# Scan passes over one image in two directions instead of two images in one, with rows repeated by single transfers from device memory

## The chip, the cores and the metric
One NeuronCore of a Trainium2 chip runs the whole program. Its engines are TensorE (PE; its weight loads are shown apart, as PEld), VectorE (DVE), ScalarE (ACT), GpSimd (POOL) and SyncE (SP), which here only issues DMAs. Each engine runs its own instructions in order, and they wait for each other on semaphores. Sixteen DMA engines serve the core. The metric is the device time of one execution in microseconds (us), and the median of several runs is compared.

## What is computed
The input is x, four images of 16 by 16 pixels with 192 channels, float32. First comes a layer with a selective scan (after a normalisation of x in groups of 6 channels), then attention with positive features over 12 heads, then a layer in which a router picks 6 of 12 heads per image; each adds to x. The scan layer is the part that changes:

```
xz = x @ in_proj_w.T;  xh, z = split(xz)             # 96 channels each
xc = silu(depthwise_conv3x3(xh) + conv_b)
xs = rows order, columns order, and both reversed    # K = 4 directions of L = 256 steps
dts, Bs, Cs = split(xs @ x_proj_w[k].T)              # 12, 16 and 16 rows
d = softplus(dts @ dt_projs_w[k].T + dt_projs_b[k])
h = h * exp(d_t * A) + (d_t * u_t) * B_t             # 96 channels x 16 states, for t = 0 .. 255
y_t = sum over states of h * C_t, plus D * u_t
y = the four directions turned back and added; then layer norm, * silu(z), @ out_proj_w.T
```

The outputs are the four images after all three layers.

## The kernel before
**Passes and units.** The scan runs in eight passes (`SCANS`), numbered n: two halves of two images each (`HALVES`, `IMG`), times the four directions. A pass holds its two images side by side, 512 columns. A unit u is a twelfth of a pass (`UNITS`): 8 channels by 16 states on the 128 partitions. There are 96 units. In unit u:
- PE's `spread_out` multiplies a 0/1 matrix with `stack` (the step d and the input d*u, each as a sum of three bf16 numbers hi, mid and lo), which repeats each channel's row over its 16 states: `step_bc` for the decay, `inp_bc` for the drive, each in two PSUM banks.
- ACT's `expo` makes the decay exp(a * d) from `step_bc` (L732), three buffers.
- DVE's `drive_of` multiplies `inp_bc` with `b_rep`, the repeated rows of B (L1010), and `scan` runs the recurrence over the 512 columns (L1019) into one of four `state` buffers.
- POOL's `weigh` multiplies the states with `c_rep` (L559), three `outp` buffers, and PE's `sum_states` adds over the states into `y_acc` (L1397). After twelve units DVE's `add_y` adds `y_acc` to `y_sum` in the direction's order (L1034, L1037, L1044).

**Preparation.** Around the start of pass n, at fixed units (`PRE_RAW` to `PRE_LO`), the next pass is prepared: PE's `pre` (L1374), ACT's `pre_raw` (L699, L704), clip on DVE (L976), exponential and logarithm on ACT (L710, L712), `pre_ln`, `pre_max` and `pre_max_series` (L980, L984, L989), the product with the input (L997), casts on ACT (`hi`, `mid`, L720, L724), subtractions on POOL (L544, L549). SP's queue copies `bc` sixteen times per pass into `b_rep` and `c_rep` (L433) and `hi`, `mid` and `lo` nine times into `stack` (L446). POOL's `orders` writes the three other directions of `xs`.

**Before the loop** the first half is normalised, projected and convolved on DVE (L955, L958), one image after the other, and gated (L962); the second half's convolution goes through PE in the loop.

**Steps beside the units.** `side_work` is a planner: it places the steps of the later layers (`ATTN_STEPS`, `HEAD_STEPS`, `FFN_STEPS`; 34 for each image) in lists `beside[u]`, by costs `PE_COST` and a room of `PE_ROOM` per unit. PE does them in unit u, the other engines one unit later (`LAG`). What doesn't fit stands in `rest` and follows the loop: image 0 and 1 may start after 48 units, images 2 and 3 after all 96. Here `rest` holds 91 steps. The steps named later: `yT` (the scan's sum turned), `q0` to `q2`, `kv00` to `kv11` (features), `hT`, `lg` and `cr` (router), `fq`, `fk`, `fv`, `s0`, `s1` (scores), `t0`, `t1` (probabilities turned), `w0`, `w1` (values weighed), `fo` and `rn` (end of an image).

```
            for u in range(SLOT_COUNT):
                expo(u)
                ...
                for item in beside[u - LAG] if u >= LAG else []:
                    side(*item)
```

Of the kernel before, what the change touches and what calls it, by code (L numbers as in the profile page):

```python
# [24 lines left out]
P = 128  # L25
IMAGES, SIDE, CH = 4, 16, 192
L = SIDE * SIDE
HALVES = 2
IMG = IMAGES // HALVES
TOK = IMG * L  # L30
TILES = TOK // P
CK = CH // 2
DI, NS, RANK, DIRS = 96, 16, 12, 4
GRP = P // NS
UNITS = DI // GRP
CHUNK = 32
CHUNKS = DI // CHUNK
PER_CHUNK = CHUNK // GRP
# [7 lines left out]
RING = 3  # L46
SLOTS = 3
STATE_SLOTS = 4
# [10 lines left out]
PRE_HI, PRE_REST, PRE_MID, PRE_LO = (2, 3), (4, 5), (5, 6), (6, 6)  # L59
SECOND_LATER = 3  # L60
LOG_MAX = 82.0

CONST2 = 3 + 1 + HPC + TOPK
ONES = 13
BEHIND = (0, 0, 0, 6)
FIRST_STEP = 4
ADD_Y = 3
Z_GATED = 2
ACC_ROWS = IMG * (SIDE + 2) - 2
SCANS = HALVES * DIRS  # L70
# [6 lines left out]
HEAD_STEPS = ["s0", "t0", "s1", "w0", "t1", "w1"]  # L77
# [17 lines left out]
def side_work():  # L95

    beside = [[] for _ in range(SLOT_COUNT)]

    for at, step in FRONT_BESIDE:
        beside[at].append((step, 1))  # L100
    for i, step in enumerate(WEIGHT_STEPS):
        beside[WEIGHTS_FIRST + 2 * i].append((step, 0))
# [3 lines left out]
    done, ready = [0, 0], [DIRS * UNITS + FIRST_STEP, DIRS * UNITS + FIRST_STEP + 1]  # L106
    for u in range(DIRS * UNITS, SLOT_COUNT):
        held = 0.0
        for n in (0, 1):
            if ready[n] > u or done[n] >= (len(steps) if n == 0 else done[0]):  # L110
                continue
            step = steps[done[n]]
            if step in HEAD_STEPS and (n % IMG or step == "w0"):
# [8 lines left out]
    at = {step: i for i, step in enumerate(steps)}  # L122
    done += [0, 0]
    rest = []
    while min(done) < len(steps):
        for n in range(IMAGES):
            if done[n] == len(steps) or (n and done[n - 1] < min(len(steps), done[n] + 1 + BEHIND[n])):
                continue
            if n >= IMG and (done[n] == at["tT"] and done[n - IMG] <= at["fv"] or done[n] == at["un"] and done[n - IMG] <= at["fo"]):
                continue  # L130
            rest.append((steps[done[n]], n))
            done[n] += 1
# [3 lines left out]
def products(step, n):  # L136
# [7 lines left out]
    if step in HEAD_STEPS:  # L144
        heads = range(int(step[1]), TOPK, 2)
        return {"s": [f"s{n}{j}" for j in heads], "t": [f"pt{n}{j}" for j in heads], "w": [f"pv{n}", f"pd{n}"] * (step == "w0")}[step[0]]
# [11 lines left out]
def ring_plan():  # L158

    beside, rest = side_work()  # L160
    names = ["w_in", "gm0", "w_xp", "w_dt", "gv0", "w_alog", "xh0_0", "xh1_0", "w_fold", "gm1", "z_0", "gv1", "d0"]
# [9 lines left out]
    for i, name in enumerate(names):  # L171
        if name[:2] in ("pv", "pd"):
            at = FINAL_RING - 2 + (name[1] == "d")
        else:
            at = turn % (RING if i < early else FINAL_RING - 2)
            turn = turn + 1 if i + 1 != early else 0
# [5 lines left out]
def hybrid_kernel(nc, x, in_proj_w, conv_w, conv_b, x_proj_w, dt_w, dt_b, A_logs, Ds, norm_g, norm_b, out_proj_w,  # L182
# [5 lines left out]
    with ExitStack() as ctx:  # L188
# [31 lines left out]

        step_bc = [ctx.enter_context(nc.psum_tensor(f"step_bc{i}", [P, TOK], F32)) for i in range(2)]
        inp_bc = [ctx.enter_context(nc.psum_tensor(f"inp_bc{i}", [P, TOK], F32)) for i in range(2)]
        y_acc = ctx.enter_context(nc.psum_tensor("y_acc", [P, TOK], F32))
        banks = [ctx.enter_context(nc.psum_tensor(f"ring{i}", [P, TOK], F32)) for i in range(RING)]
        banks += step_bc + inp_bc + [y_acc]

        def bank(name):
# [3 lines left out]
        x_tok = sb("x_tok", [P, HALVES * TILES, CH])  # L231
# [12 lines left out]
        spread = sb("spread", [DI, PER_CHUNK, P], BF16)  # L244
# [17 lines left out]
            "room_b", [([CK, 2, HALVES * TOK], F32), ([FEAT, HPC, FEAT], F32), ([FEAT, HPC, HD], F32), ([CK, HPC, FEAT], F32)],  # L262
            [([P, PAIRS, TOK], F32)])
        valr = sb("valr", [1, IMG, 3 * HEADS, HD])
        acc, opw, hn = shared("room_e", [([DI, ACC_ROWS, SIDE], F32), ([CK, 2, DI], F32)], [([P, TILES, CH], F32)])
# [3 lines left out]
                                                        ([DIRS * UNITS, P], F32)], [([P, TILES, DI], F32)],  # L269
                                             [([P, TILES, CH], F32)])  # L270
        sg, gT = shared("room_i", [([DI, TOK], F32)], [([DI, TOK], F32)])

        stack, prob1, probT1 = shared("room_s", [([DI, 2, CHUNKS, 2 * TOK], BF16)],
                                      [([P, PER_ROUND, 2, L], F32), ([P, PER_ROUND, 2, L], F32)])
        prob = [sb("prob0", [P, PER_ROUND, 2, L]), prob1]
        probT = [sb("probT0", [P, PER_ROUND, 2, L]), probT1]


        fq = [sb("fq0", [CK, 2, L])]
# [1375 lines left out]
```

## Time and profile before
| | |
|---|---|
| median of 3 runs | 461.55 us (460.12 to 461.58) |
| the profiled execution | 463.01 us, of which the profile's span is 461.3 us |
| PE, share of the span | 371.3 us, 80% |
| DVE | 346.4 us, 75% |
| POOL | 206.9 us, 45% |
| ACT | 179.8 us, 39% |
| DMA | 12.69 MB in 15743 packets, mean 28 GB/s |

The profile shows the instructions of each engine with start, duration, source line (L12 is line 12 of the kernel) and the idle time before them, with what ended it. Durations come from one execution. "State" is the scan's output, "room_g" and the like are names of shared memory: room_g holds `xs` and later results, room_s `stack`, room_a the keys' features, room_e the convolution's sums, room_i the gate, room_h and room_f inputs of steps.

### The profile page before, as it was taken

To read this page: it belongs to the slowest core of one execution; us is meant where nothing else is said; L and a number is where in the kernel's file an instruction comes from. 1 tells how busy PE (TensorE), PEld (TensorE's weight loads), DVE (VectorE), ACT (ScalarE), POOL (GpSimd) and SP (SyncE) were. 2 spreads that over 40 slices of the span, in tenths; PEclk is the share of its full clock that TensorE was granted. 3 is DMA by queue.
4 is the path that set the end of the run, shared out by engine and by line. 5 is a ranking of instruction groups with operands and counts; after the bars stand their busy time and mean duration, and the time that the engine had idled before them with its cause. 6 is when DMAs were issued, how large, how long until landed. Compare 5 with 4: busy or idle time off the path is not lost. (4 is left out here: it accounts for less than half of the span.)

```text
span 461.3 us, 5553 instructions
## 1 busy us (share of the span) xinstructions
PE 371.3 (80%) x1669; PEld 214.3 (46%) x1669; DVE 346.4 (75%) x622; ACT 179.8 (39%) x405; POOL 206.9 (45%) x210
## 2 busy tenths in 40 slices
PE   5825499697887867857999998896989999969691
PEld 4612133142332312323557555553865786958450
DVE  5885989878999999999789898987457356263514
ACT  2565354554563534423243332335225211135340
POOL 7131697867895967774653863451121010000001
PEclk9999889979897987785999999999799989588966
DMA  5502212011121110110101010000000000000000
GB/s 121 106 21 64 56 26 64 23 41 34 23 58 34 47 40 18 40 43 9 47 21 33 11 34 1 0 2 1 2 17 1 1 0 17 2 1 1 1 17 18
DMA packets 15743, 12.69 MB, mean 28 GB/s; under 512 B 7279, under 2 KB 11361, under 8 KB 15713
## 3 DMA queue, kind: packets, MB, share of 16 engines
q1 hardware_dynamic: 15713, 12.33, 11.7%
q8 instruction: 14, 0.23, 0.2%
q14 instruction: 16, 0.13, 0.1%
HBM read 2.62 MB, written 0.79 MB: 7 GB/s over the span
## 5 line engine op out<-in xcount | busy, mean ns | idle before, releaser
L559 POOL TENSOR_TENSOR outp<-state,c_rep 128x512 f32<-128x512 f32 x96 | 126.4, 1321 | 93.0 <-PE y_acc L1397 43.1
L1019 DVE TENSOR_TENSOR_SCAN state<-decay,inp_bc 128x512 f32<-128x512 f32 x96 | 117.2, 1221 | 9.3 <-DVE inp_bc L1010 4.3
L1397 PE MATMUL y_acc<-outp,band 128*96 128x512 f32 x192 | 111.2, 666 | 6.7 <-DVE y_sum L1034 2.6
L732 ACT ACTIVATE decay<-step_bc,a_neg 128x510 f32<-128x510 f32 x96 | 64.9, 683 | 47.0 <-PE step_bc L1384 46.8
L1010 DVE TENSOR_TENSOR inp_bc<-b_rep,inp_bc 128x512 f32<-128x512 f32 x96 | 65.5, 682 | 7.1 <-PE inp_bc L1388 6.9
L1388 PE MATMUL inp_bc<-room_s,spread 96*128 96x512 bf16 x96 | 41.0, 427 | 31.1 <-DVE state L1019 31.0
L494 POOL TENSOR_TENSOR rs<-mv,neg_half 128x2 f32<-128x2 f32 x16 | 11.1, 696 | 120.0 <-DVE mv L1055 119.9
L1384 PE MATMUL step_bc<-room_s,spread 96*128 96x512 bf16 x96 | 39.9, 415 | 12.7 <-DMA room_s<-lo 11.6
L1397 PEld LDWEIGHTS y_acc<-outp,band 128*96 128x96 f32 x192 | 34.3, 182 | 24.7 <-issue 10.3
L1388 PEld LDWEIGHTS inp_bc<-room_s,spread 96*128 96x128 bf16 x96 | 9.9, 103 | 65.9 <-DVE state L1019 56.8
L1384 PEld LDWEIGHTS step_bc<-room_s,spread 96*128 96x128 bf16 x96 | 10.4, 109 | 32.5 <-issue 27.3
L720 ACT CAST hi<-step 96x512 bf16<-96x512 f32 x16 | 9.9, 616 | 33.4 <-DVE step L989 24.7
L1507 PE MATMUL ring<-kvw,tT 96*128 96x480 f32 (+1 forms) x48 | 21.2, 567 | 0.0
L1132 DVE RECIPROCAL spl<-y_acc 96x256 f32<-96x256 f32 x4 | 7.0, 1754 | 15.4 <-PE y_acc L1436 15.4
L1125 DVE TENSOR_REDUCE nmax<-ring 128x2 f32<-128x512 f32 x19 | 12.0, 680 | 7.1 <-PE step_bc L1407 3.9
L1501 PE MATMUL ring<-tT,qw 96*128 96x256 f32 (+1 forms) x64 | 16.6, 404 | 0.8 <-issue 0.8
L544 POOL TENSOR_TENSOR step<-step,hi 96x512 f32<-96x512 f32 x14 | 16.1, 1151 | 0.0
L549 POOL TENSOR_TENSOR lo<-step,mid 96x512 bf16<-96x512 f32 x14 | 15.9, 1154 | 0.0
L1501 PEld LDWEIGHTS ring<-tT,qw 96*128 96x128 f32 (+1 forms) x64 | 12.8, 202 | 5.9 <-issue 4.3
L724 ACT CAST mid<-step 96x512 bf16<-96x512 f32 x16 | 9.9, 616 | 13.6 <-POOL step L544 13.4
L1525 PEld LDWEIGHTS ring<-cbd,room_b 128*128 128x128 f32 x96 | 13.7, 227 | 1.0 <-issue 1.0
L1525 PE MATMUL ring<-cbd,room_b 128*128 128x34 f32 x96 | 13.6, 307 | 0.0
(346 smaller groups left out, 650.8 us busy)
## 6 DMA issues: line engine op xcount, KB each, us to landing
b_rep<-bc SPq DMA_DIRECT2D x64, 32.0 KB, 1.9
c_rep<-bc SPq DMA_DIRECT2D x64, 32.0 KB, 2.0
room_s<-hi SPq DMA_DIRECT2D x24, 64.0 KB, 2.0
room_s<-mid SPq DMA_DIRECT2D x24, 64.0 KB, 2.0
room_s<-lo SPq DMA_DIRECT2D x24, 64.0 KB, 2.0
x_tok<-in_x_dram SPq DMA_DIRECT2D x2, 384.0 KB, 3.8
out_dram<-room_g SPq DMA_DIRECT2D x4, 192.0 KB, 2.0
room_a<-in_L_attn_w_qkv_dram SPq DMA_DIRECT2D x1, 432.0 KB, 6.5
```

Source lines behind the costliest of these rows:

```text
L544: g.tensor_tensor(step2[:, i, :], step2[:, i, :], hi[:, i, :], ALU.subtract).then_inc(S["rest"], 1)
L549: g.tensor_tensor(lo[:, i, :], step2[:, i, :], mid[:, i, :], ALU.subtract).then_inc(S["lo"], 1)
L559: g.tensor_tensor(outp[:, u % SLOTS, :], state[:, u % STATE_SLOTS, :], c_rep[:, n % 2, :], ALU.mult).then_inc(S["outp"], 1)
L732: a.activation(decay[:, u % SLOTS, :, 1:L], step_bc[u % 2][:, :].rearrange("p (b l) -> p b l", b=IMG)[:, :, 1:L], ACT.Exp, scale=a_neg[:, ...
L1010: v.tensor_tensor(inp_bc[u % 2][:, :], b_rep[:, n % 2, :], inp_bc[u % 2][:, :], ALU.mult).then_inc(S["drive"], 1)
L1019: v.tensor_tensor_scan(state[:, u % STATE_SLOTS, :], decay[:, u % SLOTS, :, :].rearrange("p b l -> p (b l)"), inp_bc[u % 2][:, :], 0.0, AL ...
L1384: t_.matmul(step_bc[u % 2][:, :], spread[:, q, :], stack[:, n % 2, j, 0:TOK], start=True, stop=True).then_inc(S["bc_step"], 1)
L1388: t_.matmul(inp_bc[u % 2][:, :], spread[:, q, :], stack[:, n % 2, j, TOK:2 * TOK], start=True, stop=True).then_inc(S["bc_inp"], 1)
L1397: t_.matmul(y_acc[0:DI, :], band[:, at:at + DI], outp[:, u % SLOTS, :], start=(g12 == 0), stop=(g12 == UNITS - 1)).then_inc(S["y_mm"], 1)
L1501: ins = t_.matmul(b_[:, u * L:(u + 1) * L], qw[0:CK + c, c, i * P:(i + 1) * P], tT[0:CK + c, c, at0:at0 + L], start=(c == 0), stop=(c == 1))
L1507: ins = t_.matmul(b_[:, 0:w], tT[0:CK + c, c, at:at + P], kvw[0:CK + c, c, j, :], start=(c == 0), stop=(c == 1))
L1525: ins = t_.matmul(b_[:, at:at + w], qp[:, i, at0 + t * P:at0 + (t + 1) * P], cbd[:, b, i, :], start=True, stop=True)
```

## The change
A pass is now one image read in row order and in column order, side by side (`WAYS`), and its two backward directions are the next pass: eight passes again, image 0 forward, image 0 backward, image 1 forward and so on. For a backward pass the decay and the scan are read from the last column to the first, and only the column order is made by `orders`. A unit is 16 channels by 8 of the 16 states (`SN`), twelve a pass again: six with the lower states, six with the upper.

The step and the input (`step2`, float32, no splitting) are written by SP's queue to `step_rows` in device memory, once a pass, and each unit's 16 rows come back by one transfer that repeats each 8 times (`in_rep`, four slots). C goes through `c_rows` likewise, two transfers a pass. B comes repeated out of a product, `fill_b`, into two banks `b_bc`. `spread_out`, `stack`, the casts and the subtractions are gone. The drive has one bank, `drv`; the decay two buffers. The ring of banks has four instead of three in the loop and all eight after it. Image n's later steps may start from unit 24(n+1)+4, and many steps wait one unit instead of two for their predecessor. `prob` and `probT` exist once instead of twice, and `w0` and `w1` are one step `w`. `rest` now holds 64 steps instead of 91.

```diff
-HALVES = 2
-IMG = IMAGES // HALVES
+IMG = 2
+WAYS = 2
-GRP = P // NS
-UNITS = DI // GRP
+SN = 8
+GRP = P // SN
+GROUPS = DI // GRP
+PARTS = NS // SN
+UNITS = PARTS * GROUPS
+PER_IMAGE = DIRS // WAYS
-RING = 3
+RING = 4
 SLOTS = 3
+IN_SLOTS = 4
+DECAY_SLOTS = 2
-BEHIND = (0, 0, 0, 6)
+BEHIND = (0, 0, 0, 0)
...
-UNITS_AFTER = {step: 1 for step in ("q0", "q1", "q2", "kv00", "kv01", "kv10", "wqk", "wv", "fq", "fk")}
+UNITS_AFTER = {step: 1 for step in ("gT", "tT", "q0", "q1", "q2", "kv00", "kv01", "kv10", "kv11", "cx", "aT", "hT", "wqk", "wv", "fq", "fk", "fv", "t0")}
...
+    ready = [PER_IMAGE * UNITS * (n + 1) + FIRST_STEP for n in range(IMAGES)]
+    for u in range(PER_IMAGE * UNITS, SLOT_COUNT):
...
+            def keep_c(n):
+                taken(sp, f"d{n}")
+                sp.dma_start(c_rows[n % 2].rearrange("i s t -> (i s) t"), step2[DI:, 0, :]).then_inc(S["c_kept"], 16)
+            def repeat_c(n, i):
+                sp.wait_ge(S["c_kept"], 16 * (n + 1))
+                if n:
+                    sp.wait_ge(S["outp"], UNITS * (n - 1) + GROUPS * (i + 1))
+                sp.dma_start(c_rep[:, i, :], c_rows[n % 2, i].unsqueeze(0).to_broadcast([GRP, SN, TOK])).then_inc(S["c_there"][i], 16)
+            def keep_step(n):
+                sp.wait_ge(S["step"], n + 1)
+                if n >= 2:
+                    sp.wait_ge(S["decay"], UNITS * (n - 1))
+                sp.dma_start(step_rows[n % 2], step2[0:DI, :, :].rearrange("p a t -> p (a t)")).then_inc(S["step_kept"], 16)
+            def repeat_step(u):
...
+                if u % UNITS == 0:
+                    sp.wait_ge(S["step_kept"], 16 * (n + 1))
+                if u >= IN_SLOTS:
+                    sp.wait_ge(S["decay"], u - IN_SLOTS + 1)
+                    sp.wait_ge(S["drive"], u - IN_SLOTS + 1)
+                rows = step_rows[n % 2, GRP * g:GRP * (g + 1), :]
+                sp.dma_start(in_rep[:, u % IN_SLOTS, :, :].rearrange("p a t -> p (a t)"),
+                             rows.unsqueeze(1).to_broadcast([GRP, SN, 2 * TOK])).then_inc(S["in_there"][u % IN_SLOTS], 16)
...
             def expo(u):
-                act.wait_ge(S["bc_step"], u + 1)
-                if u >= SLOTS:
-                    act.wait_ge(S["state"], u - SLOTS + 1)
...
+                act.wait_ge(S["in_there"][slot], 16 * (u // IN_SLOTS + 1))
+                if u >= DECAY_SLOTS:
+                    act.wait_ge(S["state"], u - DECAY_SLOTS + 1)
+                kept = slice(0, L - 1) if back else slice(1, L)
+                for e in range(WAYS):
+                    at = (part * DIRS + WAYS * back + e) * GROUPS + c16
+                    ins = a.activation(decay[:, back, u % DECAY_SLOTS, e, kept],
+                                       in_rep[:, slot, 0, :].rearrange("p (e l) -> p e l", e=WAYS)[:, e, kept],
+                                       ACT.Exp, scale=a_neg[:, at:at + 1])
...
             def drive_of(u):
...
-                dve.wait_ge(S["bc_inp"], u + 1)
-                v.tensor_tensor(inp_bc[u % 2][:, :], b_rep[:, n % 2, :], inp_bc[u % 2][:, :],
-                                ALU.mult).then_inc(S["drive"], 1)
...
+                dve.wait_ge(S["in_there"][slot], 16 * (u // IN_SLOTS + 1))
+                if u:
+                    dve.wait_ge(S["state"], u)
+                v.tensor_tensor(drv[:, :], in_rep[:, slot, 1, :], b_bc[part][:, :], ALU.mult).then_inc(S["drive"], 1)
```

**The queue of SP**, at the start of the loop. Before, from the repeats of B for the first pass on:

```order
L433 DMA b_rep<-bc 16x512 x8
L446 DMA room_s<-hi 32x1024
L446 DMA room_s<-mid 32x1024
L446 DMA room_s<-lo 32x1024
L433 DMA c_rep<-bc 16x512 x8
```

With the change, the first pass's rows and the first units:

```order
L441 DMA c_rows<-step 16x512
L455 DMA step_rows<-step 96x1024
L467 DMA in_rep<-step_rows 128x1x1024 x2
L448 DMA c_rep<-c_rows 128x1x512 x2
L467 DMA in_rep<-step_rows 128x1x1024 x5
L441 DMA c_rows<-step 16x512
L467 DMA in_rep<-step_rows 128x1x1024 x3
L455 DMA step_rows<-step 96x1024
```

The copies between parts of SBUF have become a write to device memory and one wide read a unit, and the next pass's rows are written between the reads of this one.

**PE at the end of the loop.** Before, the last unit's sums, and then the first steps of `rest` (room_e and y_sum are the inputs of hT of image 1 and yT of image 2):

```order
L1407 MATMUL ring<-fk,fq 128x256 x6
L1397 MATMUL y_acc<-outp,band 96x512 x4
L1419 MATMUL ring<-ident,prob 128x128 x12
L1447 MATMUL step_bc<-ident,room_e 96x128 x4
L1481 MATMUL step_bc<-ident,y_sum 128x96 x2
```

With the change (the scores before the loop's end are image 1's, y_sum is the input of yT of image 3):

```order
L1369 MATMUL y_acc<-outp,band 96x512
L1474 MATMUL ring<-tT,qw 128x256 x4
L1369 MATMUL y_acc<-outp,band 96x512 x3
L1391 MATMUL ring<-ident,prob 128x128 x12
L1474 MATMUL ring<-tT,qw 128x256 x4
L1454 MATMUL b_bc<-ident,y_sum 128x96 x2
```

Image 0 is finished in the loop, image 1 stands where image 0 stood, and image 2 is already at its third query product.

## Rows read from the trace of the kernel before

**Rows 1.** Stretches of the execution: length, busy time of each engine (instructions), PE clock, DMA

```profile
40.27:311.03 270.76, 227.02 (x773) 106.54 (x772) 244.48 (x335) 112.91 (x215) 178.84 (x150) 0.90 0.14 32
311.03:461.29 150.26, 124.29 (x822) 93.34 (x820) 73.42 (x210) 47.15 (x147) 13.48 (x18) 0.85 0.02 6
...
138.00:170.00 32.00, 23.96 (x65) 8.66 (x63) 31.21 (x33) 13.59 (x23) 23.35 (x19) 0.84 0.17 40
```

**Rows 2.** Timeline of DVE, units with nothing between: start, duration, line, operation

```profile
119.43 1.22 DVE L1019 TENSOR_TENSOR_SCAN state<-decay,inp_bc 128x512 f32<-128x512 f32 x1
120.57 0.68 DVE L1010 TENSOR_TENSOR inp_bc<-b_rep,inp_bc 128x512 f32<-128x512 f32 x1
121.28 1.22 DVE L1019 TENSOR_TENSOR_SCAN state<-decay,inp_bc 128x512 f32<-128x512 f32 x1
```

**Rows 3.** Waits in the loop, DVE's: us in total, times, longest

```profile
DVE inp_bc L1010 <- PE inp_bc L1388: 6.9, 8, 3.2
...
DVE state L1019 <- ACT decay L732: 2.0, 4, 1.0
```

**Rows 4.** Timeline of PE after the loop, with idle time before and its releaser

```profile
314.74 1.53 PE L1419 MATMUL ring<-ident,prob 128*128 128x128 f32 x12 [1.16 <-DVE y_sum L1044]
...
346.30 2.00 PE L1501 MATMUL step_bc<-tT,qw 96*128 96x256 f32 x8 [0.16 <-DVE room_f L1072]
```

**Rows 5.** Stretches after the loop, columns as in rows 1

```profile
311.03:346.30 35.27, 29.03 (x204) 21.72 (x202) 21.70 (x70) 12.31 (x39) 5.75 (x8) 0.90 0.02 7
346.30:461.29 114.99, 95.25 (x618) 71.62 (x618) 51.72 (x140) 34.84 (x108) 7.74 (x10) 0.83 0.02 6
```

**Rows 6.** Groups of DVE in the loop: busy us, mean ns, idle before

```profile
L984 DVE TENSOR_TENSOR step<-step,spl 96x512 f32<-96x512 f32 x7 | 10.3, 1466 | 0.0
...
L989 DVE TENSOR_TENSOR step<-step,sps 96x512 f32<-96x512 f32 x7 | 4.8, 679 | 0.0
...
L1044 DVE TENSOR_TENSOR y_sum<-y_sum,y_acc 96x256 f32<-96x256 f32 x6 | 3.2, 581 | 0.5 <-PE y_acc L1397 0.5
...
L1034 DVE SCALAR_TENSOR_TENSOR y_sum<-room_g,dsum,y_acc 96x512 f32<-96x512 f32 x2 | 1.5, 739 | 0.1
...
L1037 DVE TENSOR_TENSOR y_sum<-y_sum,y_acc 96x512 f32<-96x512 f32 x2 | 1.3, 674 | 0.0
```

**Rows 7.** The page's groups: a spread product of PE

```profile
L1388 PE MATMUL inp_bc<-room_s,spread 96*128 96x512 bf16 x96 | 41.0, 427 | 31.1 <-DVE state L1019 31.0
```

**Rows 8.** Timelines of ACT and DVE at a kv step

```profile
229.39 0.24 ACT L783 COPY v<-ring 128x96 f32<-128x96 f32 x1 [2.65 <-DVE room_a L1166]
229.53 0.69 ACT L732 ACTIVATE decay<-step_bc,a_neg 128x510 f32<-128x510 f32 x1
...
230.30 1.22 DVE L1019 TENSOR_TENSOR_SCAN state<-decay,inp_bc 128x512 f32<-128x512 f32 x1 [0.40 <-DVE inp_bc L1010]
```

**Rows 9.** Timelines of DVE and ACT before the first unit

```profile
15.93 4.10 DVE L958 SCALAR_TENSOR_TENSOR room_e<-room_w,cw,room_e 96x256 f32<-96x256 f32 x8
...
25.87 0.42 DVE L962 TENSOR_TENSOR room_g<-room_e,room_i 96x256 f32<-96x256 f32 x1 [0.40 <-ACT room_i L671]
...
34.31 1.41 DVE L1002 TENSOR_TENSOR step<-step,hi 96x512 f32<-96x512 f32 x2
...
40.27 0.69 DVE L1010 TENSOR_TENSOR inp_bc<-b_rep,inp_bc 128x512 f32<-128x512 f32 x1 [3.18 <-PE inp_bc L1388]
...
20.59 0.42 ACT L669 ACTIVATE room_i<-room_i 96x256 f32<-96x256 f32 x1
```

**Rows 10.** Short stretches at the start, columns as in rows 1

```profile
3.00:4.00 1.00, 0.00 (x0) 0.00 (x0) 0.86 (x2) 0.00 (x0) 1.00 (x3) 1.00 1.07 359
9.00:11.50 2.50, 2.27 (x12) 1.90 (x11) 0.59 (x4) 0.47 (x1) 1.05 (x2) 1.00 0.63 65
```

**Rows 11.** The page's DMA issues: count, KB each, us from issue to landing

```profile
room_s<-hi SPq DMA_DIRECT2D x24, 64.0 KB, 2.0
...
x_tok<-in_x_dram SPq DMA_DIRECT2D x2, 384.0 KB, 3.8
```

More of the change, by code:

```diff
@@ L126, in side_work @@
         for n in range(IMAGES):
[L127 to L132, printed above, removed]
+            if may_go(n):
+                rest.append((steps[done[n]], n))
+                done[n] += 1
     return beside, rest
@@ L144, in products @@
     if step in HEAD_STEPS:
-        heads = range(int(step[1]), TOPK, 2)
-        return {"s": [f"s{n}{j}" for j in heads], "t": [f"pt{n}{j}" for j in heads], "w": [f"pv{n}", f"pd{n}"] * (step == "w0")}[step[0]]
+        heads = [] if step == "w" else range(int(step[1]), TOPK, 2)
+        return {"s": [f"s{n}{j}" for j in heads], "t": [f"pt{n}{j}" for j in heads], "w": [f"pv{n}", f"pd{n}"]}[step[0]]
     return [f"{step}_{n}"]
@@ L663, in _ @@
[L663 to L674 removed]
+            act.wait_ge(S["conv"], 9)
@@ L676, in weights @@
+            for n in range(1, IMAGES):
+                group_normed(n)
+            for n in range(1, IMAGES):
+                pad(n)
             def weights(step):
@@ new lines, in collected, with group_deviations @@
+            def collected(first, last, count):
+                dve.wait_ge(S["gn_stats"], count)
+                for s in range(2 * first, 2 * last):
+                    v.bn_aggr(gmv[:, s, :], gst[:, s, :]).then_inc(S["gn_agg"], 1)
+            def group_deviations(i, cols):
+                w = cols.stop - cols.start
+                fetched(dve, f"gm{i}")
+                dve.wait_ge(S["gn_agg"], cols.stop)
+                v.tensor_copy(gmean[:, cols], bank(f"gm{i}")[0:CK, 0:w]).then_inc(freed(f"gm{i}"), 1)
+                taken(dve, f"gm{i}")
+                v.tensor_tensor(gdv[:, cols], gmv[:, cols, 0], gmean[:, cols], ALU.subtract).then_inc(S["gn_dev"], 1)
+                dve.wait_ge(S["gn_dev"], 2 * i + 1)
+                v.tensor_tensor(gsq[:, cols], gdv[:, cols], gdv[:, cols], ALU.mult).then_inc(S["gn_dev"], 1)
+                dve.wait_ge(S["gn_dev"], 2 * i + 2)
+                v.tensor_tensor(gva[:, cols], gsq[:, cols], gmv[:, cols, 1], ALU.add).then_inc(S["gn_var"], 1)
@@ L913, in _ @@
+            group_bias(0, one)
+            turned_stats(2, 1)
+            for c in range(2):
+                turned_stats(3, c)
+            collected(1, IMAGES, 2 * IMAGES)
             for e in range(2):
@@ new lines, in pre, with fill_b @@
+            def pre(n):
+                b_ = begin(f"d{n}")
+                for e in range(WAYS):
+                    ins = way(b_, n, e)
+                done(ins)
+            def fill_b(n, part):
+                if n:
+                    pe.wait_ge(S["drive"], UNITS * (n - 1) + GROUPS * (part + 1))
+                i = n // PER_IMAGE
+                pe.wait_ge(S["xs"], i + 1)
+                for e in range(WAYS):
+                    k = WAYS * (n % PER_IMAGE) + e
+                    ins = t_.matmul(b_bc[part][:, e * L:(e + 1) * L], w_b[:, k, part, :], xs[:, i, e, :], start=True, stop=True)
+                ins.then_inc(S["b_there"], 1)
@@ L1595, in side @@
                     done(ins)
-            front("z", 0)
+            for n in range(1, IMAGES):
+                inner(n)
             b_ = begin("d0")
```

803 lines of the change are left out of this document (350 added, 453 removed).

## The prediction

> **What bounds the kernel now.** I read first the three stretches into which the first and the last scan cut the execution [rows 1, 9]: 40.3 us before the first drive, 270.8 us in which the 96 units run, 150.3 us after the last scan. In the middle stretch VectorE (DVE) is busy 244.5 of 270.8 us, no other engine over 227. In the last it is busy 73.4 of 150.3 and TensorE (PE) 124.3: the loop belongs to DVE, the end to PE. The timeline of DVE shows the smallest unit: drive 0.71 us to the scan, scan 1.14 us to the next drive, 1.85 us, with the drive starting 0.08 us before the scan's end [rows 2]. 96 of these are 178 us; the rest of the loop is preparation of the next pass and steps of the later layers, woven between the units. The waits of DVE in the loop come third: 6.9 us for the bc product that PE makes, little for the decay [rows 3].
>
> **The end.** This carries the gain. Before, the layers behind the scan may start for two images only after 48 units; now image n starts after 24(n+1). What PE has left after the loop falls from 91 steps to 64 by the planner. The new list starts with the turning of image 1's probabilities, q2 of image 2 and yT of image 3. The old list reaches exactly this state (yT of image 3 just done) when PE starts q2 of image 2, at 346.30 [rows 4]. From there to the end it took 115.0 us, PE busy 95.3 of it [rows 5]. Between the last scan's end, 311.03, and PE's first step, 314.74 [rows 4], 3.7 us went into the last product, sum and add_y, which stay. I add 2 us, since fk and fv of image 3 now run with no other image's work beside them, and nothing for the changed banks. New end: 3.7 + 115.0 + 2 = 120.7, so 150.3 becomes 120.7: **-29.6 us**. Bounds: -33 (more banks let PE run on) and -22 (PE's mean granted clock was 0.83 of full speed here [rows 5]; a lower one stretches it).
>
> **The loop.** It starts and ends with the same 96 units of 128x512. Terms on DVE:
> - The steps that leave the end enter the loop. The old end did them from 311.03 to 346.30, with DVE busy 21.7 us [rows 5]; +21.7.
> - Drive u+1 now waits until scan u has finished, since there is one drv where there were two banks. An instruction that waits for its predecessor starts 0.03 us after its end (scan after drive), one that doesn't starts 0.08 before it [rows 2]: 0.12 a unit where nothing stands between. By the plan 27 of the 95 changes of unit are such; +3.3. Bounds 0 and 11.4 (all 95).
> - add_y: in the loop ten instructions, 3.2 + 1.5 + 1.3 = 6.0 us [rows 6]. Now three images by about 0.48 + 0.58: -2.8. A memset of 0.5 goes to POOL, the gate of image 1 (0.5) comes in from the start: 0.
> - PE makes no more spread products, two a unit; B comes from one product for half a pass. The 6.9 us of waits for inp_bc [rows 3] go. PE is no more near its limit: these products (96 by 0.43 us [rows 7], and 96 of the other kind, taken as equal) are some 82 of its 227 us.
> - POOL loses 28 subtractions, ACT 28 casts: neither bounds, so nothing in the sum by itself. What DVE loses to POOL is visible: the maximum with spl takes 1466 ns on average, its twin with sps 679 [rows 6], 5.5 us in all. I take that it stays, as POOL's products still run beside it.
> - ACT reads the decay's exponent from SBUF in two instructions of 255 columns. One of 256 took 0.42 [rows 9], one of 510 0.69 [rows 8]; the pair costs about 0.8, 0.1 more, and lies on the path only where ACT waits for DVE first. That is seen at the kv steps: ACT's copy waits for DVE's, the exponential comes behind it, and the scan starts 0.40 us after its drive [rows 8]. Eight such steps: +1. The same happens at the heads' scores (three maxima on DVE, six exponentials and then the decay on ACT), which come into the loop three times, and at their two weighings: +5 together, at 1 us each. Bounds 0 and 15, as decay now has two buffers and ACT can be only one unit ahead.
>
> Sum: 21.7 + 3.3 - 2.8 - 6.9 + 6 = **+21.3 us**; the loop is then 292 us, 3.04 a unit.
>
> The transfers are to hide in this. Each unit reads 16 rows of 4 KB from device memory, each eight times: 524 KB, where the passes before moved 12.7 MB in all. No row shows such a transfer. From above: loading x ran at 359 GB/s [rows 10], or 1.5 us a unit. From below: while the vectors that repeat one row over 128 partitions were loaded, 65 GB/s moved at a busy share of 0.63 [rows 10], 103 if full, or 5.1 us a unit. I take 260 GB/s, 2.0 us: here 16 different rows are read at once, one by each DMA engine, which is nearer to x than to one row for all. Then the 16 DMA engines are busy two thirds of the loop, and four buffers, freed when decay and drive are done, leave four units (7.9 us at least) for issue, landing and exponential, 5 us. Hidden, at nothing. Without this cover each us beyond the unit's own 3.04 costs 96 us. SP issues one a unit (0.5 us) in order; the repeat of C waits behind POOL's product of two units ago, done by then.
>
> **The start.** With one image instead of two before the first pass, the gate that ended at 26.29 [rows 9] ends when the first convolution (to 20.0), three exponentials and logarithms of 0.42 and one product of 0.42 are done, at 21.9: -4.4. The product of the second way now waits for POOL's reordering: +0.7. From the finished step (34.31, where the splitting starts) to the first drive (40.27) it took 5.96 us: splits on DVE, stack, spread. Now a write of 384 KB (3.0, between 2.0 for 64 KB and 3.8 for 384 KB [rows 11]), then a read of 512 KB (4.0, as the larger of these and a little), with 0.2 of waits: 7.2, +1.2. **Start -2.5 us**; bounds -5 and +2.
>
> On these two transfers the Trainium skill, "DMA: Bandwidth & Descriptors", section on measured bandwidth, would give 2.0 us and the bytes at 436 GB/s, an estimate of 2.9 and 3.2 us: the sum would be 1 us lower. By its section on latency (device memory answers in 2 us instead of 0.2 at high load) it would be some 4 us higher. No row here shows either. On the long maximum, "SBUF — State Buffer" (rules on the shared port) says that a VectorE instruction with two SBUF inputs is held up by a GpSimd one that reads SBUF; the trace agrees, 1466 against 679 ns. By that rule, with 28 POOL instructions fewer, up to 5.5 us more could go.
>
> **Sum**: -2.5 + 21.3 - 29.6 = -10.8 us. The profiled execution took 463.01 (span 461.3), so 452.2 for such a one; the median of the runs is 461.55, so **450.8 us**.
>
> **Rivals.**
> 1. *The transfers set the pace; slower.* At in_rep. It decides when 524 KB need more than 3.04 us, under 172 GB/s. At 150 GB/s a unit is 3.5 us, the loop 336, 66 more than now: 461.55 - 2.5 + 66 - 29.6 = 495 us. For it: the rows that repeat one line run at 103 GB/s when full. Against: 359 GB/s for x, in shorter runs. Chance 0.15. If writes into SBUF slowed the engines it would look alike, but the skill's SBUF page says that DMA and engines cannot contend, and no row here tells.
> 2. *The stalls go; faster still.* From 138 to 170 us DVE is busy 31.2 of 32.0 [rows 1]. With that share, work of 244.5 + 21.7 + 3.3 - 2.8 = 266.7 takes 273 us instead of 292: 432 us. For it: most idle time of DVE waits for PE's queue, which empties, and part of the 5.5 us of the long maximum can go with POOL's subtractions. Against: steps now stand one unit apart and wait for each other across engines. Chance 0.15.
> 3. *ACT and the heads eat the gain.* Decay two deep, two instructions a unit, three images' copies in the loop: with 10 to 20 us of stalls more, 461 to 471. For it: the 0.40 us at each kv step. Against: ACT is busy 113 of 271 us. Chance 0.12.
> 4. *The scan read backwards costs more.* Half of the units do so. At half as long again, 48 by 0.61 = 29 us: 480. Against: the sum that reads y_acc backwards took 674 ns for 512 columns like any other [rows 6]. Chance 0.05.
>
> **How the numbers follow.** Forecast 0.53, rivals 0.15, 0.15, 0.12, 0.05. The range takes the forecast with its bounds, rivals 2 to 4: 432 to 480. Left out are rival 1 and the edge of 2. What this measurement can tell from no change is about 0.3%, 1.4 us. Faster: 0.53 + 0.15 + 0.04 of rival 3 = 0.72; same 0.04 (rival 3); slower 0.04 + 0.15 + 0.05 = 0.24.
>
> **What would show it.** Right: last scan some 120 us before the end; 96 units in 285 to 300 us; DVE over 88% busy between; first scan at 38 to 39; drive-to-drive 1.97 us where nothing lies between; transfers landing in under 5 us, with hardly a wait for in_rep on ACT or DVE. Wrong: ACT's or DVE's waits named in_rep, in tens of us; an end that still takes 130 us or more; scans of over 1.3 us in odd passes.

## The result and the profile after

The changed kernel takes 480.94 us (median of 4 runs, 479.27 to 482.1), the kernel before in the same session 461.56 (460.12 to 463.07): ratio 1.042, 95% interval 1.037 to 1.046. It is slower by 19 us. The forecast was 450.8 us, faster; the result lies just above the upper end of the range, 480. Medians here are over all runs of a kernel; the ratios leave out slow executions, four of ten in e2_warm and two of four in e6_later, without which these two medians are 461.1 and 487.7 us.

The profiled execution took 479.27 us, of which the span is 477.5. First the stretches of the changed kernel, cut at its first drive and its last scan as in [rows 1, 5] (columns as there), with a second set of cuts inside the end:

```profile
0.00:43.63 43.63, 23.30 (x95) 17.16 (x95) 18.52 (x66) 15.30 (x37) 10.51 (x37) 0.94 0.42 90
43.63:337.42 293.79, 225.56 (x864) 129.81 (x864) 261.09 (x391) 135.94 (x344) 151.45 (x125) 0.86 0.77 194
337.42:477.50 140.08, 113.86 (x639) 85.57 (x636) 54.53 (x151) 35.25 (x108) 10.16 (x13) 0.77 0.02 5
...
337.42:348.10 10.68, 8.86 (x44) 5.79 (x41) 3.70 (x8) 3.86 (x9) 1.72 (x2) 1.00 0.00 1
348.10:477.50 129.40, 105.00 (x599) 79.78 (x598) 50.83 (x144) 31.39 (x99) 8.44 (x11) 0.75 0.02 5
```

The three stretches had been forecast at 37.8, 292 and 120.7 us. They are 43.6, 293.8 and 140.1. So the loop came out within 1.7 us, the start missed by 5.9 us and the end by 19.4. Together that is 27.0 of the 30.1 us between 450.8 and 480.94; the rest lies in which executions were profiled, above the median before (463.01) and below it after (479.27).

**The loop.** DVE is busy 261.1 of 293.8 us (0.89). The timeline of DVE, where nothing stands between units, answers to [rows 2] (L991 is the drive now, L1002 the scan):

```profile
90.68 0.70 DVE L991 TENSOR_TENSOR drv<-in_rep,b_bc 128x512 f32<-128x512 f32 x1
91.41 1.22 DVE L1002 TENSOR_TENSOR_SCAN state<-decay,drv 128x512 f32<-128x512 f32 x1
92.73 0.70 DVE L991 TENSOR_TENSOR drv<-in_rep,b_bc 128x512 f32<-128x512 f32 x1
93.46 1.22 DVE L1002 TENSOR_TENSOR_SCAN state<-decay,drv 128x512 f32<-128x512 f32 x1
```

A drive now starts 0.10 to 0.11 us behind the scan's end and a bare unit takes 2.05 us, not 1.97. All 96 scans, backward or forward, take the same: the next row gives smallest, median and largest in ns. The rows under it are DVE's and ACT's longest waits in the loop, as in [rows 3].

```profile
L1002 DVE TENSOR_TENSOR_SCAN state<-decay,drv x96: 1219/1220/1222, 44.6 to 336.2; 128x512 f32<-128x512 f32 x96
```

```profile
DVE state L1002 <- DVE drv L991: 6.7, 10, 1.0
DVE state L1002 <- ACT decay L731: 5.9, 8, 2.4
...
ACT decay L731 <- DVE state L1002: 54.3, 35, 5.0
...
ACT decay L731 <- DMA in_rep<-step_rows: 25.1, 13, 11.2
```

Of ACT's 25.1 us for in_rep, 11.2 are the very first unit. The reads of a unit landed 5.0 us after their issue (median, the page's DMA issues):

```profile
in_rep<-step_rows SPq DMA_DIRECT2D x96, 512.0 KB, 5.0
```

**The start.** The gate ends at 22.63 us (forecast 21.9). The first steps are then late: timelines of PE and of ACT.

```profile
23.90 4.89 PE L1256 MATMUL ring<-room_b,room_f 96*96 96x256 f32 x12 [5.82 <-ACT room_b L630]
28.63 1.03 PE L1342 MATMUL ring<-xs,pre_w 96*112 96x256 f32 x4
```

```profile
24.55 1.01 ACT L630 ACTIVATE room_b<-y_acc,gbi,grs 96x256 f32<-96x256 f32 x2
...
28.88 0.37 ACT L616 COPY room_c<-ring 96x256 f32<-96x256 f32 x1 [0.82 <-PE ring L1256]
29.69 0.83 ACT L708 ACTIVATE step<-ring,dtb 96x256 f32<-96x256 f32 x2 [0.44 <-PE ring L1342]
```

The product of the first pass (`d0`, L1342) stands on PE behind the projections of images 1 to 3 (L1256), and on ACT its copy (L708) stands behind their normalisation and their copies.

**The end.** The mean granted clock of PE is 0.75 of full speed from 348.10 on, where it was 0.83 over the same steps in the kernel before. Short windows show two levels, 1.00 and 0.50, and that it stays at the lower one for long:

```profile
346.00:366.00 20.00, 17.73 (x115) 10.34 (x114) 12.35 (x35) 5.85 (x17) 2.68 (x4) 1.00 0.00 1
366.00:379.00 13.00, 13.00 (x56) 12.23 (x56) 1.90 (x6) 1.06 (x3) 0.99 (x1) 0.50 0.04 15
380.00:391.00 11.00, 10.85 (x47) 6.86 (x44) 6.67 (x20) 1.79 (x7) 0.70 (x1) 1.00 0.00 0
394.00:416.00 22.00, 22.00 (x88) 18.78 (x89) 3.27 (x13) 2.19 (x12) 0.00 (x0) 0.50 0.00 0
```

What PE did before the first fall is in its timeline:

```profile
361.74 1.78 PE L1480 MATMUL ring<-kvw,tT 96*128 96x480 f32 x4
365.46 4.77 PE L1488 MATMUL b_bc<-v,room_a 128*128 128x34 f32 x24 [1.94 <-ACT v L780]
370.04 1.07 PE L1417 MATMUL b_bc<-ident,room_h 128*96 128x128 f32 x4
370.92 5.30 PE L1498 MATMUL drv<-cbd,room_b 128*128 128x34 f32 x24
376.03 3.76 PE L1474 MATMUL y_acc<-tT,qw 96*128 96x256 f32 x8
```

PE paused for 1.94 us, waiting for ACT's copy of v ahead of `cx` of image 2, and then 24 products of 34 columns took 4.77 us. (`cx`, L1488, multiplies the keys' features with v into the attention's context; `at`, L1498, multiplies the queries' features with that; `cr`, L1528, turns the router's values.) In the kernel before this step came without a pause and took 2.87 us:

```profile
366.30 2.87 PE L1515 MATMUL step_bc<-v,room_a 128*128 128x34 f32 x24
```

The second long stretch at the lower level, from 394, follows a pause of 1.73 us ahead of `cr` of image 2. Four shorter ones, the last from 458 us, come the same way, each behind a pause of 0.85 to 2.04 us.

### The profile page after: what moved, and what is told of

It is laid out like the page before. It is cut to its first block and busy times, and to the rows that moved or that the text cites. A ratio compares the mean times of both kernels' runs of the same rounds, so it can differ in the third digit from the quotient of the medians.

```text
span 477.5 us, 5515 instructions
## 1 busy us (share of the span) xinstructions
PE 362.7 (76%) x1595; PEld 232.5 (49%) x1595; DVE 334.1 (70%) x606; ACT 186.5 (39%) x489; POOL 172.1 (36%) x174
## 5 line engine op out<-in xcount | busy, mean ns | idle before, releaser
L1002 DVE TENSOR_TENSOR_SCAN state<-decay,drv 128x512 f32<-128x512 f32 x96 | 117.2, 1220 | 16.7 <-DVE drv L991 6.7
L731 ACT ACTIVATE decay<-in_rep,a_neg 128x255 f32<-128x255 f32 x192 | 86.2, 503 | 79.8 <-DVE state L1002 54.3
L991 DVE TENSOR_TENSOR drv<-in_rep,b_bc 128x512 f32<-128x512 f32 x96 | 66.1, 688 | 12.7 <-DMA in_rep<-step_rows 10.1
L534 POOL TENSOR_TENSOR rs<-mv,neg_half 128x2 f32<-128x2 f32 x16 | 11.2, 698 | 146.0 <-DVE mv L1029 146.0
L1359 PEld LDWEIGHTS b_bc<-xs,w_b 96*128 96x128 f32 x64 | 13.9, 217 | 10.4 <-issue 8.4
L1359 PE MATMUL b_bc<-xs,w_b 96*128 96x256 f32 x64 | 18.7, 421 | 0.0
L1391 PE MATMUL ring<-ident,prob 128*128 128x128 f32 x76 | 13.8, 332 | 6.3 <-ACT prob L752 3.7
L1391 PEld LDWEIGHTS ring<-ident,prob 128*128 128x128 f32 x76 | 10.8, 172 | 10.6 <-ACT prob L752 5.3
L616 ACT COPY room_c<-ring 128x512 f32<-128x512 f32 (+1 forms) x23 | 11.7, 566 | 10.5 <-PE ring L1391 5.6
L1430 PE MATMUL ring<-room_c 96*96 96x256 f32 x54 | 13.0, 381 | 1.5 <-ACT qw L616 1.0
L1535 PE MATMUL ring<-sel_m,fT 96*96 96x96 f32 (+1 forms) x64 | 10.1, 342 | 5.0 <-DVE sel_u L1178 5.0
```

What stands on the lines that cost most here:

```text
L731: ins = a.activation(decay[:, back, u % DECAY_SLOTS, e, kept], in_rep[:, slot, 0, :].rearrange("p (e l) -> p e l", e=WAYS)[:, e, kept], AC ...
L991: v.tensor_tensor(drv[:, :], in_rep[:, slot, 1, :], b_bc[part][:, :], ALU.mult).then_inc(S["drive"], 1)
L1002: v.tensor_tensor_scan(state[:, u % STATE_SLOTS, :][:, order], held[:, order], drv[:, :][:, order], 0.0, ALU.mult, ALU.add).then_inc(S["st ...
L1359: ins = t_.matmul(b_bc[part][:, e * L:(e + 1) * L], w_b[:, k, part, :], xs[:, i, e, :], start=True, stop=True)
L1391: ins = t_.transpose(b_[:, (2 * kt + q) * P:(2 * kt + q + 1) * P], prob[:, j // 2, q, kt * P:(kt + 1) * P], idn)
L1430: ins = t_.matmul(b_[0:DI, 0:L], taps[:, i, :], xpad[:, n, i // 3:i // 3 + SIDE, i % 3:i % 3 + SIDE], start=(i == 0), stop=(i == 8))
```

## The experiments

The theory after this reading: the end missed because PE's pauses let the clock fall (the order of the steps leaves a pause just ahead of long stretches of narrow products), and the start missed because of the order of two queues. The rivals: the clock falls with the narrow products, whatever stands ahead of them; the transfers hold the loop; the moved steps gain nothing.

**Order of the start.** `names` is the order in which PE makes the products ahead of the loop; `inner(n)` is the projection of image n (`xh_n`).

```diff
-    names = [..., "w_fold", "xh_1", "xh_2", "xh_3", "d0"]
+    names = [..., "w_fold", "d0", "xh_1", "xh_2", "xh_3"]
...
-            for n in range(1, IMAGES):
-                inner(n)
             b_ = begin("d0")
...
+            for n in range(1, IMAGES):
+                inner(n)
             pe.wait_ge(S["const2"], CONST2)
```

On ACT `pre_raw(0)` and `pre_softplus(0)` likewise go ahead of `group_normed` and `pad` of images 1 to 3, on POOL the clearing of wsel behind `orders(0)`.

> The product of the first step (d0) and ScalarE's copies of it go ahead of the projections and normalisations of images 1 to 3, and GpSimd's clearing of wsel behind the reordering of image 0. If the start is long because the first pass waits behind the other images' work in the queues of PE and ACT: the first drive moves from 43.6 to about 38 us, loop (293.8) and end (140.1) stay, 475 to 476 us. Rival, the moved work is paid in the first units: first drive at 38, but a loop of 297 to 300, 479 to 481 us.

475.12 us (473.0 to 475.79), 5.8 us less by the medians. First drive at 39.2 (some 38 had been expected), loop 294.8, end 140.1. PE makes the first pass's product 5.4 us earlier than in the changed kernel:

```profile
23.26 2.02 PE L1342 MATMUL ring<-xs,pre_w 96*112 96x256 f32 x4 [4.72 <-DVE xs L950]
```

The first drive comes 4.4 us earlier. In the other runs here that leave the start's order alone it comes at 43.6 to 45.4 us, so this gain is clear of that spread.

**Pauses filled.** `warm` repeats a product of `ident` with itself into the bank that the step has just taken; the step's own product, or transpose, overwrites it.

```diff
+            WARM = {"cx_2": 9, "cr_2": 8, "cx_3": 4, "cr_3": 9, "pt20": 4, "pt30": 8, "pt31": 8}
+
+            def warm(b_, name):
+                for _ in range(WARM.get(name, 0)):
+                    t_.matmul(b_[:, 0:P], ident[:], ident[:], start=True, stop=True)
```

> 50 products of 128x128 more on PE, in seven places after the loop where it waits (cx and cr of images 2 and 3, the turned probabilities t0 of image 2, t0 and t1 of image 3); their results are overwritten. If the clock falls to half because PE pauses there: mean granted clock after the last scan rises from 0.77 to 0.88 or more, the end shrinks from 140 to 123 to 132 us, 464 to 473 us in all. Rival, the clock falls with the narrow products (cx, at, 34 columns) whatever precedes them: clock 0.75 to 0.80, the added products cost 3 to 10 us, 483 to 491 us.

462.34 us (median of 10 runs, 456.25 to 467.91), 18.6 us less than without, for 50 products more; a little better than the range expected. The stretches of this kernel:

```profile
44.90:337.10 292.20, 227.03 (x864) 130.69 (x864) 259.30 (x391) 135.81 (x344) 151.54 (x125) 0.85 0.77 195
337.10:460.00 122.90, 105.13 (x739) 79.25 (x736) 54.39 (x151) 34.44 (x108) 10.19 (x13) 0.94 0.02 6
...
394.00:416.00 22.00, 20.11 (x169) 17.70 (x168) 6.42 (x20) 8.33 (x32) 0.69 (x1) 1.00 0.01 2
```

The end is 122.9 us instead of 140.1, and its clock 0.94 instead of 0.77. PE's timeline at the same place:

```profile
363.06 2.17 PE L1235 MATMUL b_bc<-ident 128*128 128x128 f32 x18
365.16 2.84 PE L1497 MATMUL b_bc<-v,room_a 128*128 128x34 f32 x24
367.83 0.62 PE L1424 MATMUL b_bc<-ident,room_h 128*96 128x128 f32 x4
368.69 5.00 PE L1507 MATMUL drv<-cbd,room_b 128*128 128x34 f32 x24 [0.23 <-ACT cbd L787]
```

`cx` starts when it did (365.16 against 365.46) and takes 2.84 instead of 4.77 us. One fall is left while PE still has work, from 369, inside the narrow products of `at`, with no more than 0.23 us of pause ahead of it. So part of the rival is true: narrow products can drop the clock without a pause.

**The same work in other places.** As a control, the table became `{"kv00_2": 9, "q0_3": 8, "q2_3": 4, "kv00_3": 9, "fk_2": 4, "fq_3": 8, "fk_3": 8}`, again 50 products.

> The same 50 products of 128x128 as in e2_warm, but ahead of steps of the end before which PE does not wait (kv00, q, fq, fk of images 2 and 3), so that the pauses stay. If what holds the clock up is that the pauses are filled: clock of the end 0.74 to 0.82 as without them, the end 140 plus 8 to 15 us, 485 to 496 us in all. Rival, any additional work of PE in the end holds the clock up: 0.88 or more, 464 to 475 us.

485.52 us (482.57 to 489.01):

```profile
340.50:487.20 146.70, 120.69 (x739) 94.28 (x736) 54.55 (x151) 35.37 (x108) 10.21 (x13) 0.81 0.02 5
```

The end is 146.7 us at a clock of 0.81 (148 to 155 had been expected). The number of products does not hold the clock; their place does. The pauses of 1.94, 1.73, 0.85, 2.10, 1.70 and 1.74 us stand where they were and a fall follows each; one more, at 410 us, comes at the end of `cx` of image 3 with no pause ahead of it. What this pair of runs does not separate is a pause filled from wide products put directly ahead of narrow ones: in e2_warm the same products do both.

**The kernel before, with its pauses filled**: `{"cr_1": 14, "cx_3": 4, "cr_3": 9, "pt30": 10}`.

> The kernel before the change, with 37 such products where its PE pauses in the end (cr of images 1 and 3, cx of image 3, t0 of image 3). If pauses drop the clock here too: clock of the end from 0.85 to 0.92 or more, end from 150 to 140 to 145 us, 451 to 456 us in all. Rival, its falls come otherwise (one of them, at 374.8, had no pause before it): 460 to 466 us.

455.89 us (453.08 to 458.04), ratio to the kernel before 0.985 (0.981 to 0.989):

```profile
309.30:454.40 145.10, 126.68 (x896) 95.97 (x894) 73.37 (x210) 46.45 (x147) 13.51 (x18) 0.90 0.02 6
```

The end is 145.1 us. So the kernel before lost to the clock at its pauses as well, but less: 5 us of its end against 17. Its clock stays below the 0.92 expected: of the four falls left before PE's last steps, three, at 365, 372 and 389 us, come inside or right behind products of 34 columns, with no pause ahead of them.

**Half of the bytes.**

```diff
-                rows = step_rows[n % 2, GRP * g:GRP * (g + 1), :]
+                w = 2 * TOK if u < IN_SLOTS else TOK
+                rows = step_rows[n % 2, GRP * g:GRP * (g + 1), 0:w]
```

> Leaves out: from the fifth unit on, only the step's half of each row comes back (256 KB a unit instead of 512), the drive reads stale input rows. If the transfers are hidden but for some waits of ACT: loop 290 to 294, 477 to 481 us. Rival, the transfers hold the loop (by their landing, or by taking SBUF from the engines): loop 280 to 287 us, 467 to 475 us in all.

476.59 us (476.5 to 478.27). The loop in the profile:

```profile
45.00:337.20 292.20, 226.83 (x864) 130.68 (x864) 258.36 (x391) 135.78 (x344) 152.25 (x125) 0.84 0.36 113
```

The DMA share fell from 0.77 to 0.36 and the loop stayed at 292.2, the same as in e2_warm, which moves all bytes. The transfers are hidden; the rival's 280 to 287 did not come. The median is 4 us lower than the changed kernel's; the profiles show 1.6 us of it in the loop and 0.8 in the end, and the start 1.4 longer, so where the rest lies stays open.

**Later starts.** `ready`, the unit from which an image's steps may start, counts from `PER_IMAGE * UNITS * (n + 2)` instead of `(n + 1)`.

> Each image's later steps may start 24 units later than in the changed kernel, 92 steps remain after the loop instead of 64, about as many as before (91). If the price of the moved steps was sized right (21.7 us of DVE and about 5 of stalls in the loop, 29.6 at the end): loop 268 to 275, end 163 to 172 us, 480 to 488 us in all. Rival, starting earlier gives nothing or costs, since the end is set by waits and the clock and not by the number of steps: end 145 to 155, 462 to 474 us in all.

491.41 us (486.89 to 505.61), ratio to the kernel before 1.057 where the changed kernel has 1.042:

```profile
43.80:304.70 260.90, 191.53 (x653) 99.42 (x656) 239.35 (x323) 131.03 (x316) 148.09 (x119) 0.85 0.88 218
304.70:485.20 180.50, 145.67 (x853) 107.62 (x847) 75.19 (x218) 41.63 (x136) 14.23 (x18) 0.80 0.02 5
```

Loop 260.9, end 180.5: both further out than expected. The 28 steps cost 32.9 us in the loop and save 40.4 at the end, so the earlier start is worth about 7 us, not the 3 that 29.6 less 26.7 gives. The rival, an end of 145 to 155, falls.

This run also stands next to the kernel before, which leaves 91 steps behind the loop where this one leaves 92. Its loop is 9.9 us shorter [rows 1], its end 30.2 us longer: PE is busy 145.7 us there instead of 124.3, at a clock of 0.80 instead of 0.85, and idle 34.8 instead of 26.0. So the loop is cheaper with the new units when about as many steps stand in it, and the new end is dearer for about as many steps. The clock is part of that; what the single `prob` buffer, the banks or the order of the images have in it, no run tells.

**Three buffers for the decay** (`DECAY_SLOTS = 3`).

> Three buffers for the decay instead of two. If ACT being one unit ahead costs what DVE's waits for the decay show (5.9 us): loop 288 to 291 instead of 293.8, 475 to 479 us in all. Rival, the wait moves to the drive or to in_rep: loop 293 to 295, 480 to 482 us.

478.58 us (476.82 to 479.36), loop 292.0. The time lies in the range expected, the loop does not (288 to 291). Over the kernels here that leave the units alone, the loop took 291.3 to 295.7 us, so this tells no gain. DVE's wait for the decay is 7.4 us with three buffers, 5.9 with two: a third buffer did not shorten it.

**The drive in SBUF.**

```diff
-                if u:
-                    dve.wait_ge(S["state"], u)
-                v.tensor_tensor(drv[:, :], in_rep[:, slot, 1, :], b_bc[part][:, :], ALU.mult).then_inc(S["drive"], 1)
+                if u > 1:
+                    dve.wait_ge(S["state"], u - 1)
+                v.tensor_tensor(drvs[:, u % 2, :], in_rep[:, slot, 1, :], b_bc[part][:, :], ALU.mult).then_inc(S["drive"], 1)
```

> The drive goes to two buffers in SBUF instead of one PSUM bank, so that it no longer waits for the scan before it. If the wait for the single bank is a term of the loop of its own: drive to drive 1.85 us where nothing lies between (2.05 now), loop 287 to 291 instead of 293.8, 475 to 479 us. Rival, with both inputs of the scan in SBUF, where GpSimd's product reads too, the scans take longer than 1.22 us: loop 296 to 320, 483 to 507 us.

506.57 us (504.64 to 508.71), loop 321.8, at the rival's upper end and past it. All scans, and a stretch of DVE's timeline:

```profile
L1003 DVE TENSOR_TENSOR_SCAN state<-decay,drvs x96: 1223/1578/2362, 45.6 to 364.9; 128x512 f32<-128x512 f32 x96
```

```profile
92.99 1.58 DVE L1003 TENSOR_TENSOR_SCAN state<-decay,drvs 128x512 f32<-128x512 f32 x1
94.49 0.65 DVE L992 TENSOR_TENSOR drvs<-in_rep,b_bc 128x512 f32<-128x512 f32 x1
95.18 1.82 DVE L1003 TENSOR_TENSOR_SCAN state<-decay,drvs 128x512 f32<-128x512 f32 x1
```

The wait is gone (a drive starts 0.08 us before the scan's end again), but the scans take 1.60 us on average instead of 1.22. The Trainium skill, "SBUF — State Buffer" (section "Who interferes with whom"), says that a VectorE instruction with two SBUF inputs contends with a GpSimd one that reads SBUF. This run agrees: by the timelines of DVE and POOL, the 22 scans that ran beside no GpSimd instruction took 1.22 to 1.23 us, the 74 others 1.71 on average. The single PSUM bank costs 0.2 us a bare unit, the drive in SBUF 0.38 us a scan.

**The first rows written in two parts.** `step_rows` of channels 0 to 15 is written first, and the first unit waits for that part alone.

> The first pass's rows are written in two parts, the first 16 channels ahead, so that the first unit's read starts before the rest is written. If the write's bytes are the term: the first drive 1 to 2 us earlier (42 to 43 instead of 43.6), 479 to 480 us in all. Rival, the fixed time of a transfer sets it, or the second part holds up the read: first drive at 43.5 to 45, 481 to 482 us.

478.62 us (476.89 to 482.18). From the end of the last step's product to the first drive it took 7.1 us instead of 7.9: DVE's wait for in_rep was 7.06, before 7.91. The first drive came at 43.60 all the same, as the step was ready 0.8 us later in this execution. The gain is at most that 0.8 us. How the 7.1 us that are left divide into write and read, this run does not tell.

**All that helped.** e1_start and e2_warm together, and on PE:

```diff
-                for item in beside[u]:
+                for item in beside[u] if u + 1 < SLOT_COUNT else []:
                     side(*item)
             for u in range(SLOT_COUNT - Y_LAG, SLOT_COUNT):
                 sum_states(u)
+            for item in beside[SLOT_COUNT - 1]:
+                side(*item)
```

> e1_start and e2_warm together, and the later steps of the last unit placed behind the last three sums on PE, so that the turned y starts sooner. If the three parts are independent: first drive at 39, loop 293 to 295, end 119 to 123 us, 453 to 457 us in all, faster than both kernels. Rival, the clock loses elsewhere what one part gains (the clock's falls are not the same from order to order): 460 to 468 us.

456.92 us (median of 10, 455.03 to 460.57), ratio to the kernel before 0.9895 (0.986 to 0.993). First drive 39.2, loop 295.7, end 123.5, the last two 0.7 and 0.5 us above what was expected. From the last scan's end to `t0` of image 1 it is 6.3 us instead of 7.3. Two falls of the clock were left, at 366 within the 34-column products of `at` of image 2 and at 401 right behind those of image 3. So the next kernel adds `"at_2": 6, "at_3": 6` to the table.

> e8_all with six more products of 128x128 each ahead of at of images 2 and 3, whose own products have 34 columns and in whose stretch the clock still fell to half without a pause before it (366 to 376 us and 401 to 403 in e8_all). If wide products ahead of the narrow ones hold it up: end 117 to 121 us instead of 123.5, 451 to 455 us in all. Rival, the narrow products drop the clock by themselves, or the added work costs as much: 456 to 460 us.

454.5 us (453.79 to 455.2), ratio 0.983 (0.981 to 0.985): the fastest here. Its end and the place of the fall:

```profile
333.70:453.50 119.80, 103.36 (x763) 78.22 (x760) 54.47 (x151) 34.44 (x108) 10.15 (x13) 0.96 0.02 6
```

```profile
363.86 1.50 PE L1235 MATMUL drv<-ident 128*128 128x128 f32 x12
365.19 2.77 PE L1506 MATMUL drv<-cbd,room_b 128*128 128x34 f32 x24
367.79 1.98 PE L1482 MATMUL y_acc<-tT,qw 96*128 96x256 f32 x8
```

`at` takes 2.77 us, where it took 5.00 in e2_warm, and the query product behind it 1.98 instead of 3.76. No fall is left before PE's last steps.

The stretches of all kernels, in us, from one profiled execution each, beside the medians:

| kernel | first drive | loop | end | clock of the end | median |
|---|---|---|---|---|---|
| before | 40.3 | 270.8 | 150.3 | 0.85 | 461.56 |
| before, pauses filled | 40.3 | 269.0 | 145.1 | 0.90 | 455.89 |
| changed | 43.6 | 293.8 | 140.1 | 0.77 | 480.94 |
| e1_start | 39.2 | 294.8 | 140.1 | 0.77 | 475.12 |
| e2_warm | 44.9 | 292.2 | 122.9 | 0.94 | 462.34 |
| e9_ctrl | 44.9 | 295.6 | 146.7 | 0.81 | 485.52 |
| e8_all | 39.2 | 295.7 | 123.5 | 0.92 | 456.92 |
| e10_wide | 39.2 | 294.5 | 119.8 | 0.96 | 454.5 |

## Why the prediction was wrong

**The end** (forecast -29.6, measured -10.2). The step that failed is "From there to the end it took 115.0 us" taken over as a duration. The work was the same: behind yT and q2, to the end, PE was busy 93.5 us at a clock of 0.83 before, which is 77.6 us at full clock, and 105.0 at 0.75 after, 78.8. It is the clock that was carried over wrongly. I had named it as a bound ("a lower one stretches it", -22) and not seen that the order of the steps decides it. The 19.4 us are 5.2 from the last scan to 348.10 (10.7 us where 3.7 and q2's 1.8 had been taken: q1 of image 2 ahead of the last sums, and t0 of image 1), and 16.2 in what follows (11.6 more of PE's busy time, of which some 10 are the clock, and 4.6 more of idle time), less the 2 that I had added. So the clock is about half of the miss; the steps ahead of yT and the idle time, taken over as they were before, are the other half, and were not tried alone. With the pauses filled the end took 122.9 and 119.8 us, next to the 120.7 forecast, but that is luck: their clock was 0.94 and 0.96, not the 0.83 that the forecast carried with it. At 0.83 the changed kernel's end would be some 130 us, an estimate from its 140.1 less those 10. That the clock's falls hang on where PE pauses and what it does behind the pause, and not on how much it does, is shown by e2_warm against e9_ctrl; that narrow products have their own part in it, by e10_wide.

**The start** (forecast -2.5, measured +3.4). The step that failed is "the gate ... at 21.9: -4.4", which I let run through to the first drive. It was true of the gate (22.63) and not of what waits for it: between the gate and the first pass stood, in two in-order queues, the work of images that had been in no hurry. Moving it gave 4.4 us at the first drive. The two transfers were sized 7.2 and took 7.9, and the gate itself came 0.7 late. The two other estimates for the transfers, 1 us lower and some 4 higher, were further off.

**The loop** (forecast +21.3, measured +23.0). The sum is right in part by luck, since two terms missed in opposite directions. The wait for the single drive bank costs 0.20 us a bare unit, not 0.12, by 1.85 and 2.05 us. DVE's busy time is 261.1, 5.6 less than 266.7: the long maximum took 877 ns on average over its eight (1369 before), against my "I take that it stays", and the clip 404 instead of 839; the product for `spl` took 1002 instead of 740. These averages hide single long instructions: the maximum took 2.35 us three times before and once after, each time beside GpSimd's product with C and never beside a subtraction, and 0.66 at the shortest. So it is a matter of where the two meet, which nobody tried alone. Idle time is 32.7 us instead of 25.3.

**The rivals.** Rival 1 fell: half the bytes, same loop. Its price was not tested; the reads kept up at 0.77 of the DMA engines' time, some 250 GB/s when full (194 by 0.77), near the 260 taken. Rival 2 did not come: DVE is busy 0.89 of the loop and not 0.975, and ACT and DVE still wait for each other. Rival 3 named the loop, where 1.7 us were lost and not 10 to 20. Rival 4 fell, 1220 ns backward and forward. Missing was the rival that decided: a lower clock in the end. The kernel before already had rows for it, a pause of PE in its timeline and the clock in the stretch behind it:

```profile
322.97 1.68 PE L1555 MATMUL step_bc<-ident,valr 1*96 1x1 f32 x12 [3.11 <-DVE valr L1115]
```

```profile
323.00:330.00 7.00, 6.91 (x41) 6.84 (x42) 2.61 (x13) 2.12 (x4) 0.59 (x1) 0.53 0.01 4
```

**What the change is worth.** With the pauses filled in both, 461.1 against 455.9 us, it is still slower: the end gives back 22 us, the loop takes 23 and the start 5. What the loop takes is mostly the moved steps, which cost DVE there about what they cost at the end: in e6_later, with 28 steps fewer in the loop, DVE is busy 21.7 us less there and 20.7 more at the end. With the start's order and the narrow stretches mended too, it reaches 454.5, level with the kernel before with its pauses filled. That kernel did not get this second round, and its clock stayed at 0.90 with three falls that no pause precedes; how the two compare with the same care was not measured.

## What to carry to other kernels

A duration taken over from another kernel's trace carries that trace's clock with it: compare PE's busy time multiplied by the granted clock, and ask of the new order where PE pauses and what stands behind the pause. Where PE bounds a stretch, filling its pauses of some 2 us with products that are thrown away gave back 5 and 17 us here; the same products in other places cost 5. When work is taken from ahead of a critical chain, follow the chain through each in-order queue: it gains only if nothing else stands before it.

## What had not been expected of the hardware

- PE's clock fell to half (1.2 GHz of 2.4) behind pauses of only 0.85 to 2.0 us and stayed there through 13 and 22 us in which PE was busy without a gap, mostly with narrow products (34 and 96 columns); both times it rose within products of 256 columns. A pause of 1.8 us at 343, between wide products, was followed by no fall. It also fell with no pause over 0.23 us, inside 34-column products (e2_warm), and 1.5 us of 128-column products ahead of them kept it up (e10_wide). The kernel before has two more such falls, at 374.6 and 391.7 us, the first behind 34-column products and the second inside them:

```profile
374.07 3.26 PE L1501 MATMUL ring<-tT,qw 96*128 96x256 f32 x8
...
391.61 5.32 PE L1525 MATMUL ring<-cbd,room_b 128*128 128x34 f32 x24
```

- A scan with both inputs in SBUF took 1.22 to 2.36 us, 1.60 on average and 1.71 where GpSimd worked beside it; with one input in PSUM 1.22 always, in every kernel here.
- Reading 16 rows eight times each from device memory moved 194 GB/s at a busy share of 0.77, where the vectors repeated over 128 partitions had moved 65 at 0.63 [rows 10].
